# Projection and Gram product as pairs of 64-row matmuls, and gathers that also wait for the slot in front

## The chip, the core and the metric

The kernel runs on one core of a Trainium2 chip, in float32 throughout. The metric is the device time of one execution in microseconds (us), with all inputs in HBM at the start and the 512 outputs in HBM at the end. Five engines work side by side, each through its own list of instructions and tied to the others by semaphores: PE (TensorE, matmuls), DVE (VectorE), ACT (ScalarE), POOL (GpSimd, which issues the gathers here) and SP (SyncE, which issues the other DMAs).

## What is computed

A recommendation tower on 512 samples. For each sample 26 embedding rows of 64 numbers are gathered, projected to 128, normalised, mixed over the 26 features into 32, normalised again, and multiplied pairwise with each other and with a projected dense vector. The products pass a linear layer and an MLP.

```python
e = jnp.stack([tbl_f[ids[:, f]] for f in range(26)], axis=1)        # (512, 26, 64)
x = layer_norm(dense_t @ Wd.T, gd, bd)                              # (512, 128)
y = layer_norm(jnp.einsum('bnd,ed->bne', e, Ws), gs, bs)            # (512, 26, 128)
y = jnp.einsum('bne,pn->bep', y, Wsi)                               # (512, 128, 32)
y = jnp.swapaxes(layer_norm(y, gsi, bsi), 1, 2)
T = jnp.concatenate([x[:, None, :], y], axis=1)                     # 33 rows of 128
Z = jnp.einsum('bnd,bmd->bnm', T, T)                                # lower triangle kept
z = layer_norm(Z[:, TRIL_I, TRIL_J] @ Wl.T, gl, bl)                 # 384 of 512 used
h = relu(concat([z, dense_t]) @ W_top1 + b_top1)
out = relu(h @ W_top2 + b_top2) @ W_top3
```

## The kernel before

The 512 samples are four chunks of 128, a chunk is four slots of 32 samples (16 slots in all, numbered s = 0 to 15). A slot's embedding rows lie in `e_rows` as 4 tiles of 128 rows (slots 0, 4, 8, 12) or 3 tiles (the others). A row of a tile holds two embeddings side by side, a and b (64 numbers each, from samples 16 apart), so that 128 columns are two halves of 64. Each tile takes two gathers on POOL (L373), one for each half: 8 or 6 per slot, 104 in all.

A slot goes through these steps, named by their function:

- `turn` (PE, L432) transposes the slot's tiles into `turn_ps`; `save_cols` (ACT, L673) copies them to `e_cols`.
- `quad` (PE, L451) multiplies `e_cols` by `gram`, a 128x128 matrix with the same 64x64 block twice on its diagonal; `variance_n` (DVE, L882 and L885) multiplies by `e_rows` and sums, which is the norm's variance without the projection itself. `root_n` (ACT, L684) and `norm_n` (DVE, L906 and L910) make `e_unit`.
- `mix` (PE, L440) mixes the features into `mix_ps` (a in partitions 0 to 63, b in 64 to 127); `save_f` (ACT, L680) copies each half to partitions 0 to 63 of its own `f_sb` buffer. Partitions 64 and up of `f_sb` hold a constant, written once, and `proj_w` has the bias in row 64 and zeros below.
- `project` (PE, L474), in the round after, multiplies each half by `proj_w` over all 128 rows: two matmuls of 512 columns into the two banks of `proj_ps`. `square` (ACT, L665), `variance_p` (DVE, L873), `root_p` (ACT, L688), `invert_p` and `norm_p` (DVE, L889 and L897) write the normalised result to `feats`.
- `dots` (PE, L465), one round later still, makes the pairwise products in 32 groups of columns; `save_z` (ACT, L704) stores them. After a chunk SP sends them through HBM back as `z_pairs`, and `linear` (L488) and the MLP follow in later rounds, between the steps above.

Round i of PE is `turn(i)`, `project(i-1)` and `quad(i)` (the two projections stand on either side of `quad`), some work of the linear layers, `mix(i)`, more of that work, `dots(i-2)`. ACT and DVE walk through their lists in the same rounds. All orders are written out by hand. On POOL, the gathers of slot s stand behind `after_round(s-2)`: for s of 4 and more it waits until `dots(s-4)` is done, which is the last thing that PE does in round s-2; for s = 2 and 3 it waits for `mix(s-2)` and for the rows of slot s-1.

The functions named in the diff, with the line numbers of the profile:

## Time and profile before

| | |
|---|---|
| time, median of 3 runs | 193.77 us (193.14 to 194.11) |
| the profiled execution, its own time | 194.12 us |
| its span in the trace | 192.2 us |
| busy in the span: PE / DVE / ACT / POOL | 148.4 / 99.7 / 89.6 / 101.6 us |
| instructions | 4178 |

The span is from the first to the last recorded instruction; about 2 us of the time lie around it. Busy time overlaps between engines, and a share of busy time doesn't say what the end waits for. For that the chain of waits and the timeline are read.

### The profile page before, as it was taken

How to read it: one execution, taken by the hardware profiler on the slowest of the kernel's cores; microseconds unless marked ns; L12 is line 12 of the kernel's file. 1: busy time of each engine (PE TensorE's matmuls, PEld its weight loads, DVE VectorE, ACT ScalarE, POOL GpSimd, SP SyncE). 2: the span in 40 equal slices, each digit the busy share in tenths (PEclk: the TensorE clock that was granted, in tenths of full speed). 3: DMA queues.
4: the chain of work that ended last, by engine and by line, in shares of the span. 5: the costliest groups of instructions: out<-in, count | busy, mean ns of one | idle time of the engine just before them, and what ended most of it. 6: DMA issues, size and time to landing. Idle time of an engine off the chain costs nothing.

```text
span 192.2 us, 4178 instructions
## 1 busy us (share of the span) xinstructions
PE 148.4 (77%) x1644; PEld 96.9 (50%) x1644; DVE 99.7 (52%) x192; ACT 89.6 (47%) x225; POOL 101.6 (53%) x113
## 2 busy tenths in 40 slices
PE   0496496958767976488869867798695889989995
PEld 0343444534444643354457646455565566446674
DVE  2390946684916882838073847361838456541001
ACT  3613043744512566755545436436744546641251
POOL 4777364757874487676375774776757720000000
PEclk9999669999979999969999999999999999999999
DMA  5813131416311015431011155111011640025000
GB/s 143 272 30 76 34 110 26 127 26 211 116 28 22 10 27 129 72 55 27 9 21 20 30 139 80 31 34 20 20 24 27 156 66 3 3 65 106 6 3 0
DMA packets 20260, 11.58 MB, mean 60 GB/s; under 512 B 12945, under 2 KB 17681, under 8 KB 20242
## 3 DMA queue, kind: packets, MB, share of 16 engines
q1 hardware_dynamic: 16226, 7.83, 15.2%
q0 software_dynamic: 3328, 3.41, 10.0%
q8 instruction: 13, 0.21, 0.5%
q10 hardware_dynamic: 688, 0.08, 0.3%
q14 instruction: 5, 0.04, 0.1%
HBM read 9.15 MB, written 2.16 MB: 59 GB/s over the span
## 4 chain that ended last, share of the span: by engine, by line
PE 40%; POOL 20%; DMA 13%; DVE 11%; issue 9%; ACT 5%; SPq 1%; POOLq 1%; DVEq 0%; ACTq 0%
POOL e_rows L373 20%; DMA e_rows<-table_dram,rows_sb 7%; PE mix_ps L440 7%; PE o_ps L488 5%; PE quad_ps L451 5%; PE proj_ps L474 4%; DMA dense_sb<-dense_t_dram 3%; DVE e_unit L910 3%; DVE e_prod L882 3%; DVE var_n L885 3%; PE dots_ps L465 3%; PE turn_ps L432 2%; PE o_ps L403 2%; PE dots_ps L396 2%; PE o_turn_ps L403 2%
## 5 line engine op out<-in xcount | busy, mean ns | idle before, releaser
L373 POOL DMA_INDIRECT e_rows<-table_dram,rows_sb x104 | 100.7, 968 | 53.1 <-issue 27.7
L440 PE MATMUL mix_ps<-mixw_sb,e_unit 128*128 128x192 f32 (+4 forms) x128 | 23.0, 325 | 17.0 <-DVE e_unit L910 17.0
L440 PEld LDWEIGHTS mix_ps<-mixw_sb,e_unit 128*128 128x128 f32 x128 | 20.0, 199 | 25.6 <-DVE e_unit L910 25.6
L882 DVE TENSOR_TENSOR e_prod<-quad_ps,e_rows 128x384 f32<-128x384 f32 (+1 forms) x16 | 9.5, 591 | 45.2 <-PE quad_ps L451 45.2
L474 PE MATMUL proj_ps<-f_sb,proj_w 128*128 128x512 f32 x60 | 32.5, 625 | 0.0
L873 DVE TENSOR_REDUCE var_p<-y_sq 128x16 f32<-128x512 f32 x32 | 20.5, 677 | 1.6 <-ACT y_sq L665 1.6
L451 PEld LDWEIGHTS quad_ps<-gram,e_cols 128*128 128x128 f32 x104 | 14.5, 206 | 12.2 <-ACT e_cols L673 11.2
L680 ACT COPY f_sb<-mix_ps 64x512 f32<-64x512 f32 x32 | 18.5, 578 | 4.5 <-PE mix_ps L440 4.1
L665 ACT ACTIVATE y_sq<-proj_ps 128x512 f32<-128x512 f32 x30 | 17.7, 589 | 5.9 <-PE proj_ps L474 5.7
L432 PE MATMUL turn_ps<-small_sb,e_rows 128*128 128x128 f32 x52 | 9.7, 302 | 13.9 <-DMA e_rows<-table_dram,rows_sb 13.8
L897 DVE TENSOR_TENSOR feats<-proj_ps,rstd_p 128x512 f32<-128x512 f32 x30 | 19.3, 686 | 0.6
L488 PE MATMUL o_ps<-wl_gained,z_pairs 128*128 128x512 f32 (+1 forms) x40 | 18.8, 600 | 0.3 <-DMA z_pairs<-z_dram 0.3
L451 PE MATMUL quad_ps<-gram,e_cols 128*128 128x128 f32 x104 | 15.7, 293 | 1.9 <-ACT e_cols L673 1.9
L684 ACT ACTIVATE std_n<-var_n,eps 128x8 f32<-128x8 f32 x16 | 4.8, 300 | 23.5 <-DVE var_n L885 23.5
L432 PEld LDWEIGHTS turn_ps<-small_sb,e_rows 128*128 128x128 f32 x52 | 6.1, 149 | 17.3 <-DMA e_rows<-table_dram,rows_sb 15.1
L465 PEld LDWEIGHTS dots_ps<-feats 128*32 128x32 f32 x1024 | 10.8, 109 | 7.3 <-issue 5.4
L688 ACT ACTIVATE std_p<-var_p,eps 128x32 f32<-128x32 f32 x16 | 5.1, 322 | 18.0 <-DVE var_p L873 18.0
L673 ACT COPY e_cols<-turn_ps 128x384 f32<-128x384 f32 (+1 forms) x16 | 8.1, 506 | 11.6 <-PE turn_ps L432 11.5
L465 PE MATMUL dots_ps<-feats 128*32 128x33 f32 x1024 | 12.7, 199 | 0.0
L488 PEld LDWEIGHTS o_ps<-wl_gained,z_pairs 128*128 128x128 f32 (+1 forms) x40 | 7.1, 190 | 7.5 <-issue 6.4
L910 DVE TENSOR_TENSOR e_unit<-e_rows,rstd_n 128x384 f32<-128x384 f32 (+1 forms) x16 | 9.6, 597 | 0.6
L885 DVE TENSOR_REDUCE var_n<-e_prod 128x6 f32<-128x384 f32 (+1 forms) x16 | 9.4, 586 | 0.6
(142 smaller groups left out, 172.8 us busy)
## 6 DMA issues: line engine op xcount, KB each, us to landing
z_dram<-z_mine SPq DMA_DIRECT2D x4, 512.0 KB, 3.2
e_rows<-table_dram,rows_sb POOLq DMA_INDIRECT x104, 2.5
w_sb<-w_dram SPq DMA_DIRECT2D x2, 512.0 KB, 6.6
wl_sb<-wl_dram SPq DMA_DIRECT2D x2, 512.0 KB, 3.4
w_sb<-w_dram SPq DMA_DIRECT2D x1, 768.0 KB, 4.2
dense_sb<-dense_t_dram SPq DMA_DIRECT2D x1, 512.0 KB, 5.8
wl_sb<-wl_dram SPq DMA_DIRECT2D x1, 256.0 KB, 2.7
z_pairs<-z_dram SPq DMA_DIRECT2D x4, 64.0 KB, 2.0
```

Of the source, the lines that this page charges most:

```text
L373: pool.indirect_dma_start(out=e_rows[:, chunk, t, D * ab:D * (ab + 1)], out_offset=None, in_=table, in_offset=bass.IndirectOffsetOnAxis(ap ...
L432: mm = pe.transpose(turn_ps[:, P * t:P * (t + 1)], e_rows[:, chunk, t0 + t, :], eye_sb)
L440: mm = pe.matmul(mix_ps[:, PR * at:PR * (at + number)], e_unit[:, t, :], mixw_sb[:, t, lo:lo + number, :].rearrange("k b p -> k (b p)"), s ...
L451: mm = pe.matmul(quad_ps[:, P * t:P * (t + 1)], e_cols[:, q % 2, P * t:P * (t + 1)], gram[:], start=True, stop=True)
L465: mm = pe.matmul(dots_ps[PR * k:PR * (k + 1), (PR + 1) * g:(PR + 1) * (g + 1)], f[:, 2:PR + 2], f[:, 0:PR + 1], start=True, stop=True)
L474: pe.matmul(proj_of(s, ab), proj_w[:], f_sb[:, q % 2, ab, :], start=True, stop=True).then_inc(projected, 1)
L488: mm = pe.matmul(o_ps[:], z_pairs[0:tall, chunk, c, :, :].rearrange("p k g -> p (k g)"), wl_gained[0:tall, c, :], start=(c == 0), stop=(c ...
L665: act.activation(y_sq[:, QB * ab:QB * (ab + 1), :].rearrange("p b q -> p (b q)"), proj_of(s, ab), ACT.Square).then_inc(sq_ready, 1)
L680: act.copy(f_sb[0:D, q % 2, ab, :], mix_ps[D * ab:D * (ab + 1), :]).then_inc(f_ready, 1)
L873: dve.tensor_reduce(var_p[:, QB * ab:QB * (ab + 1)], y_sq[:, QB * ab:QB * (ab + 1), :], AX.X, ALU.add).then_inc(ssq_ready, 1)
L897: dve.tensor_tensor(feats[:, q % 2, QB * ab:QB * (ab + 1), 2:PR + 2], proj_of(s, ab).rearrange("p (b q) -> p b q", q=PR), rstd_p[:, QB * a ...
L910: dve.tensor_tensor(e_unit[:, t0:t0 + nt, :].rearrange("p t (a d) -> p (t a) d", d=D), e_rows[:, chunk, t0:t0 + nt, :].rearrange("p t (a d ...
```

## The change

The two halves a and b are kept in different partitions throughout, so that each is multiplied over 64 rows of the array and needs no zeros:

- `save_f` becomes one copy of 128 partitions. `project` is two matmuls over partitions 0 to 63 and 64 to 127, side by side in the program, ahead of `quad`. Since no row is left for the bias, it is put into the banks first and the matmuls add to it (`start=False`): the new `seed(s)` on ACT copies the constant `y_seed` into both banks of `proj_ps` once `norm_p(s-1)` has read them, and `project(s)` waits for that. For slot 0, two matmuls with the identity do it.
- `quad` is two matmuls of 64 columns per tile, half a into `quad_ps` and half b into `turn_ps`; `variance_n` reads them in two products, and `turn` waits for these.
- The last slot's projection goes to `proj_ps` as the others, behind `dots(14)`. The setup has fewer small copies and fills.
- On POOL, the gathers of every slot from 4 on wait, beside `dots`, for the rows of the slot in front to have landed.

```diff
-        f_sb = sb("f_sb", [P, 2, 2, 512])
+        f_sb = sb("f_sb", [P, 2, 512])
+        y_seed = sb("y_seed", [P, 512])
...
@@ gpsimd
                 elif i >= 0:
                     pool.wait_ge(mixed, i + 1)
-                    pool.wait_ge(gathered[0][i + 1], 32 * tiles_of(i + 1)[1])
+                if i >= 0:
+                    chunk, q = place(i + 1)
+                    pool.wait_ge(gathered[chunk][q], 32 * tiles_of(q)[1])
...
@@ tensor, turn
                 wait(pe, cols_ready, s)
+                wait(pe, prod_done, s)
...
@@ tensor, quad
                 for t in range(nt):
-                    mm = pe.matmul(quad_ps[:, P * t:P * (t + 1)], e_cols[:, q % 2, P * t:P * (t + 1)], gram[:],
-                                   start=True, stop=True)
+                    for ab in range(2):
+                        half = slice(D * ab, D * (ab + 1))
+                        mm = pe.matmul(quad_half_ps[ab][:, D * t:D * (t + 1)], e_cols[half, q % 2, P * t:P * (t + 1)],
+                                       gram[half, :], start=True, stop=True)
                 mm.then_inc(quad_done, 1)
...
-            def project(s, ab):
+            def project(s):
+
                 _, q = place(s)
-                if s < SLOTS - 1:
-                    wait(pe, y_ready, 2 * s - 1 + ab)
-                pe.wait_ge(f_ready, 2 * s + ab + 1)
-                pe.matmul(proj_of(s, ab), proj_w[:], f_sb[:, q % 2, ab, :], start=True,
-                          stop=True).then_inc(projected, 1)
+                pe.wait_ge(f_ready, s + 1)
+                if s == 0:
+                    pe.wait_ge(prep_act, 7)
+                    for ab in range(2):
+                        pe.matmul(proj_ps[:, ab, :], eye_sb, y_seed[:], start=True, stop=True)
+                wait(pe, seeded, 2 * s)
+                for ab in range(2):
+                    half = slice(D * ab, D * (ab + 1))
+                    pe.matmul(proj_ps[:, ab, :], proj_w[half, :], f_sb[half, q % 2, :], start=False, stop=True,
+                              skip_group_check=True).then_inc(projected, 1)
...
@@ tensor, rounds
                 turn(i)
                 if i >= 1:
-                    project(i - 1, 0)
+                    project(i - 1)
                 quad(i)
-                if i >= 1:
-                    project(i - 1, 1)
...
             linear(CHUNKS - 2, range(1, 2))
-            project(last, 0)
-            project(last, 1)
             dots(last - 1)
+            project(last)
             linear(CHUNKS - 2, range(2, KZ))
...
@@ scalar
-                for ab in range(2):
-                    act.copy(f_sb[0:D, q % 2, ab, :], mix_ps[D * ab:D * (ab + 1), :]).then_inc(f_ready, 1)
+                act.copy(f_sb[:, q % 2, :], mix_ps[:]).then_inc(f_ready, 1)
+
+            def seed(s):
+
+                for ab in range(2):
+                    act.wait_ge(y_ready, 2 * (s - 1) + ab + 1)
+                    act.copy(proj_ps[:, ab, :], y_seed[:]).then_inc(seeded, 1)
...
                 if i == 10:
                     relu_2_early(0)
+                if i >= 1:
+                    seed(i)
                 if 2 <= i < SLOTS - 2:
                     save_z(i - 2)
...
             save_f(last)
+            seed(last)
             square(last, 0)
...
@@ vector, variance_n
-                dve.tensor_tensor(e_prod[:, 0:2 * nt, :].rearrange("p a d -> p (a d)"), quad_ps[:, 0:P * nt],
-                                  e_rows[:, chunk, t0:t0 + nt, :].rearrange("p t d -> p (t d)"), ALU.mult).then_inc(prod_done, 1)
+                for ab in range(2):
+                    last_prod = dve.tensor_tensor(e_prod[:, 0:2 * nt, :].rearrange("p (t a) d -> p a t d", a=2)[:, ab, :, :],
+                                           quad_half_ps[ab][:, 0:D * nt].rearrange("p (t d) -> p t d", d=D),
+                                           e_rows[:, chunk, t0:t0 + nt, D * ab:D * (ab + 1)], ALU.mult)
+                last_prod.then_inc(prod_done, 1)
```

PE's row for round 2, before. `turn_ps` is the transpose's bank, `proj_ps` the projection's, and the names in brackets are the semaphores waited for:

```order
L432 MATMUL turn_ps<-small_sb,e_rows 128x128 [waits cols_ready,gathered0_2]
L432 MATMUL turn_ps<-small_sb,e_rows 128x128 x2
L474 MATMUL proj_ps<-f_sb,proj_w 128x512 [waits f_ready,y_ready]
L451 MATMUL quad_ps<-gram,e_cols 128x128 [waits var_ready,cols_ready]
L451 MATMUL quad_ps<-gram,e_cols 128x128 x2
L474 MATMUL proj_ps<-f_sb,proj_w 128x512 [waits f_ready,y_ready]
L440 MATMUL mix_ps<-mixw_sb,e_unit 128x96 [waits f_ready,unit_ready]
```

The same place now:

```order
L431 MATMUL turn_ps<-small_sb,e_rows 128x128 [waits prod_done,cols_ready,gathered0_2]
L431 MATMUL turn_ps<-small_sb,e_rows 128x128 x2
L481 MATMUL proj_ps<-f_sb,proj_w 128x512 [waits seeded,f_ready]
L481 MATMUL proj_ps<-f_sb,proj_w 128x512
L452 MATMUL quad_ps<-gram,e_cols 128x64 [waits var_ready,cols_ready]
L452 MATMUL turn_ps<-gram,e_cols 128x64
...
L439 MATMUL mix_ps<-mixw_sb,e_unit 128x96 [waits f_ready,unit_ready]
```

The second projection has moved ahead of `quad`, `quad` has twice the matmuls, and the wait for `y_ready` has become one for `seeded`, which stands on ACT behind `y_ready`.

ACT's row from the end of round 7 into round 8, before (`o_sq`, `o_std` and `o_unit` normalise the linear layer's output of a chunk, and `e_cols` is `save_cols(8)`):

```order
L680 COPY f_sb<-mix_ps 64x512 [waits projected,mixed]
L680 COPY f_sb<-mix_ps 64x512
L727 ACTIVATE o_sq,o_var<-o_ps 128x512 [waits o_done]
L731 ACTIVATE o_std<-o_var,eps 128x1 [waits osq_done]
L735 ACTIVATE o_unit<-o_ps,o_rstd 128x384 [waits orstd_done]
L704 COPY z_mine<-dots_ps 128x33x8 [waits dotted]
L673 COPY e_cols<-turn_ps 128x512 [waits quad_done,turned]
```

And now:

```order
L678 COPY f_sb<-mix_ps 128x512 [waits projected,mixed]
L731 ACTIVATE o_sq,o_var<-o_ps 128x512 [waits o_done]
L735 ACTIVATE o_std<-o_var,eps 128x1 [waits osq_done]
L739 ACTIVATE o_unit<-o_ps,o_rstd 128x384 [waits orstd_done]
L684 COPY proj_ps<-y_seed 128x512 [waits y_ready] x2
L708 COPY z_mine<-dots_ps 128x33x8 [waits dotted]
L672 COPY e_cols<-turn_ps 128x512 [waits quad_done,turned]
```

Two copies of 64 partitions are one of 128, and two new copies stand between `o_unit` and the copy of the next slot's transposes.

POOL's gathers of slots 4 to 7, before:

```order
L373 DMA e_rows<-table_dram,rows_sb 128x64 [waits dotted]
L373 DMA e_rows<-table_dram,rows_sb 128x64 x7
L373 DMA e_rows<-table_dram,rows_sb 128x64 [waits dotted]
L373 DMA e_rows<-table_dram,rows_sb 128x64 x5
L373 DMA e_rows<-table_dram,rows_sb 128x64 [waits dotted]
L373 DMA e_rows<-table_dram,rows_sb 128x64 x5
```

And now (`gathered1_0` counts what has landed of chunk 1's first slot, slot 4):

```order
L371 DMA e_rows<-table_dram,rows_sb 128x64 [waits gathered0_3,dotted]
L371 DMA e_rows<-table_dram,rows_sb 128x64 x7
L371 DMA e_rows<-table_dram,rows_sb 128x64 [waits gathered1_0,dotted]
L371 DMA e_rows<-table_dram,rows_sb 128x64 x5
L371 DMA e_rows<-table_dram,rows_sb 128x64 [waits gathered1_1,dotted]
L371 DMA e_rows<-table_dram,rows_sb 128x64 x5
```

The first gather of each slot has one more semaphore to wait for.

## Rows read from the trace of the kernel before

**Rows 1.** The waits: engine, line, releaser: us in total, times, longest.

```profile
POOL e_rows L373 <- PE dots_ps L465: 17.6, 10, 4.2
PE turn_ps L432 <- DMA e_rows<-table_dram,rows_sb: 13.8, 10, 2.9
```

**Rows 2.** The timeline of POOL: start, us, operation; gathers at ends of slots 6 to 8.

```profile
71.17 0.94 POOL L373 DMA_INDIRECT e_rows<-table_dram,rows_sb  x1 [0.30 <-issue]
72.42 0.94 POOL L373 DMA_INDIRECT e_rows<-table_dram,rows_sb  x1 [0.30 <-issue]
...
78.66 0.94 POOL L373 DMA_INDIRECT e_rows<-table_dram,rows_sb  x1 [0.30 <-issue]
80.47 0.94 POOL L373 DMA_INDIRECT e_rows<-table_dram,rows_sb  x1 [0.86 <-PE dots_ps L465]
...
89.41 0.94 POOL L373 DMA_INDIRECT e_rows<-table_dram,rows_sb  x1 [0.30 <-issue]
```

**Rows 3.** The instructions of line 373: time from issue to landing.

```profile
DMA to landing us min/median/max: 2.3/2.5/3.6
```

**Rows 4.** The timeline of PE, round 6 and the start of round 7.

```profile
73.66 0.55 PE L432 MATMUL turn_ps<-small_sb,e_rows 128*128 128x128 f32 x3 [1.91 <-DMA e_rows<-table_dram,rows_sb]
74.04 1.02 PE L474 MATMUL proj_ps<-f_sb,proj_w 128*128 128x512 f32 x2
74.90 0.83 PE L451 MATMUL quad_ps<-gram,e_cols 128*128 128x128 f32 x6
...
78.14 1.36 PE L440 MATMUL mix_ps<-mixw_sb,e_unit 128*128 128x96 f32 x8 [1.54 <-DVE e_unit L910]
79.43 0.77 PE L465 MATMUL dots_ps<-feats 128*32 128x33 f32 x64
82.26 0.90 PE L432 MATMUL turn_ps<-small_sb,e_rows 128*128 128x128 f32 x3 [2.07 <-DMA e_rows<-table_dram,rows_sb]
```

**Rows 5.** Groups by line and form: count, busy us, mean ns, idle before.

```profile
L474 PE MATMUL proj_ps<-f_sb,proj_w 128*128 128x512 f32 x60 | 32.5, 625 | 0.0
L451 PE MATMUL quad_ps<-gram,e_cols 128*128 128x128 f32 x104 | 15.7, 293 | 1.9 <-ACT e_cols L673 1.9
L680 ACT COPY f_sb<-mix_ps 64x512 f32<-64x512 f32 x32 | 18.5, 578 | 4.5 <-PE mix_ps L440 4.1
L440 PE MATMUL mix_ps<-mixw_sb,e_unit 128*128 128x64 f32 x16 | 3.2, 287 | 1.4 <-DVE e_unit L910 1.4
L882 DVE TENSOR_TENSOR e_prod<-quad_ps,e_rows 128x384 f32<-128x384 f32 x12 | 6.7, 558 | 30.2 <-PE quad_ps L451 30.2
L882 DVE TENSOR_TENSOR e_prod<-quad_ps,e_rows 128x512 f32<-128x512 f32 x4 | 2.8, 692 | 15.0 <-PE quad_ps L451 15.0
```

**Rows 6.** The timeline of ACT and of PE in round 2.

```profile
36.84 0.47 ACT L673 COPY e_cols<-turn_ps 128x384 f32<-128x384 f32 x1
37.36 0.94 PE L451 MATMUL quad_ps<-gram,e_cols 128*128 128x128 f32 x6
```

**Rows 7.** The timeline of ACT in round 8: the copy of the transposes.

```profile
95.21 0.60 ACT L673 COPY e_cols<-turn_ps 128x512 f32<-128x512 f32 x1
```

**Rows 8.** The timeline of PE: the transposes of slots 4, 8, 12 and 15.

```profile
54.64 0.96 PE L432 MATMUL turn_ps<-small_sb,e_rows 128*128 128x128 f32 x4 [2.90 <-DMA e_rows<-table_dram,rows_sb]
...
93.85 0.63 PE L432 MATMUL turn_ps<-small_sb,e_rows 128*128 128x128 f32 x4
...
131.44 0.66 PE L432 MATMUL turn_ps<-small_sb,e_rows 128*128 128x128 f32 x4 [0.54 <-DMA e_rows<-table_dram,rows_sb]
...
157.44 0.55 PE L432 MATMUL turn_ps<-small_sb,e_rows 128*128 128x128 f32 x3 [0.74 <-DMA e_rows<-table_dram,rows_sb]
```

**Rows 9.** Granted clock (PEclk) from 51 to 58 us, and PE's projection there.

```profile
51.00:58.00 7.00, 4.10 (x69) 2.81 (x56) 2.40 (x3) 2.31 (x5) 5.48 (x6) 0.78 0.16 33
...
55.39 1.92 PE L474 MATMUL proj_ps<-f_sb,proj_w 128*128 128x512 f32 x2
```

**Rows 10.** The timeline of ACT in the tail: the last slot's second square.

```profile
166.21 0.60 ACT L665 ACTIVATE y_sq<-quad_ps 128x512 f32<-128x512 f32 x1 [0.26 <-PE quad_ps L474]
```

More of the change, by code:

```diff
@@ L151, in tower @@
         moment_ps = o_ps[0:TALL, :]
+        quad_half_ps = [quad_ps, turn_ps]
         h1_early_ps = [o_turn_ps, o_turn_ps, quad_ps]
@@ L157, in tower @@
         y_last_ps = dots_ps[0:1, 0:P]
-        proj_last_ps = [turn_ps[:], quad_ps[:]]
         ids_sb = sb("ids_sb", [P, 2, CHUNKS * TILES * 2], I32)
@@ L380, in _ @@
             pe.wait_ge(small_in, 16)
-            pe.wait_ge(consts, 5)
+            pe.wait_ge(consts, 3)
             pe.wait_ge(prep_dve, 2)
@@ L601, in _ @@
             turn(last)
-            project(last - 1, 0)
+            project(last - 1)
             quad(last)
-            project(last - 1, 1)
             dots(last - 2)
@@ L634, in _ @@
             act.wait_ge(prep_pe, 1)
-            for half in range(2):
-                for ab in range(2):
-                    last = act.copy(f_sb[D:P, half, ab, :].rearrange("p (b q) -> p b q", q=PR),
-                                    quad_ps[D:P, 0:PR].unsqueeze(1).to_broadcast([P - D, QB, PR]))
-            last.then_inc(prep_act, 1)
+            act.activation(y_seed[:].rearrange("p (b q) -> p b q", q=PR), quad_ps[:, 0:PR].unsqueeze(1).to_broadcast([P, QB, PR]),
+                           ACT.Copy, scale=bs_sb[:, 0:1]).then_inc(prep_act, 1)
             act.wait_ge(prep_pe, 2)
             act.copy(ws_rows[:], turn_ps[:, 0:D].unsqueeze(1).to_broadcast([P, 2, D])).then_inc(prep_act, 1)
-            act.activation(ws_grows[:], turn_ps[:, 0:D], ACT.Copy, scale=gs_sb[:, 0:1]).then_inc(prep_act, 1)
+            act.activation(ws_grows[:], turn_ps[:, 0:D].unsqueeze(1).to_broadcast([P, 2, D]), ACT.Copy,
+                           scale=gs_sb[:, 0:1]).then_inc(prep_act, 1)
             act.wait_ge(prep_pe, 3)
-            act.copy(gram[0:D, 0:D], mix_ps[0:D, 0:D])
-            act.copy(gram[D:P, D:P], mix_ps[D:P, 0:D]).then_inc(prep_act, 1)
+            act.copy(gram[:], mix_ps[:, 0:D]).then_inc(prep_act, 1)
             act.wait_ge(prep_pe, 4)
-            act.copy(proj_w[D:D + 1, :], ws_sb[D:D + 1, :])
-            act.copy(proj_w[0:D, :], o_turn_ps[0:D, 0:EW]).then_inc(prep_act, 1)
+            act.copy(proj_w[:], o_turn_ps[:, 0:EW]).then_inc(prep_act, 1)
             act.wait_ge(prep_pe, 5)
@@ L665, in square @@
                 act.activation(y_sq[:, QB * ab:QB * (ab + 1), :].rearrange("p b q -> p (b q)"),
-                               proj_of(s, ab), ACT.Square).then_inc(sq_ready, 1)
+                               proj_ps[:, ab, :], ACT.Square).then_inc(sq_ready, 1)
             def save_cols(s):
@@ L1037 @@
     put("eye", np.eye(P, dtype=np.float32))
-    put("ws", np.concatenate([a["L0_rec_Ws"].T, a["L0_rec_bs"][None]]))
+    put("ws", a["L0_rec_Ws"].T)
     put("wsi", a["L0_rec_Wsi"].T)
     put("gs", columns(a["L0_rec_gs"]))
+    put("bs", columns(a["L0_rec_bs"]))
     put("gd", columns(a["L0_rec_gd"]))
```

24 lines of the change are left out of this document (10 added, 14 removed).

## The prediction

> **What bounds the kernel now.** I read the chain that ended last, the waits, and then the timelines of POOL, PE and ACT round by round. The chain passes from POOL to DMA to PE and back in nearly every slot, and what ties them is a loop. POOL waits ten times for `dots`, 17.6 us in all, and PE's `turn` waits ten times for landed rows, 13.8 us [rows 1]. So neither engine is the bound alone: the gathers of slot s start when PE ends round s-2, and PE's round s starts when they have landed.
>
> The lengths in this loop: a gather takes 1.25 us from start to start, so 6 of them span 6.24 us (72.42 to 78.66) and 8 span 8.94 (80.47 to 89.41) [rows 2]. The last lands 2.5 us after its start, 3.6 at most [rows 3]; slot 7's were such, issued at 78.66 and used at 82.26 [rows 2, 4]. A light round of PE is 6.5 us long: `turn` at 73.66, `dots` over at 80.20, and then 2.07 us of waiting for rows [rows 4]. What lies in the round between `quad` and `mix` is DVE's and ACT's work on the variance, not PE's.
>
> **The wait on POOL.** At present the gathers of slot 7 start 1.25 us after the last gather of slot 6 (71.17, 72.42), those of slot 8 1.81 us after the last of slot 7 [rows 2]. With the new wait this gap can't be under landing and wake-up. POOL starts 0.27 us after the `dots` that releases it (80.20 to 80.47) [rows 2, 4], so the gap is 2.5 + 0.3 = 2.8 us, or 3.9 where the landing takes 3.6. What is queued behind this wait is all of the slot's gathers, and `turn` waits for these. The shortest period of a slot becomes 6.3 + 2.8 = 9.1 us with 3 tiles, 8.9 + 2.8 = 11.7 with 4, and about 1.1 more after a slow landing (slots 7 and 11, while `z_pairs` is read). Nothing hides it: issue and landing used to overlap between slots and no longer do. This floor is hit wherever PE's round is shorter, which light rounds of 6.5 us are.
>
> **The projection.** Two records of 512 columns take 0.86 us (74.04 to 74.90), once per half [rows 4]. The trace has no 64-row matmul. Bounds for the pair: 0.86 us if they run side by side, 1.72 if one after the other. The nearest row is `dots`, 32 matmuls into four separate column groups: 64 records in 0.77 us [rows 4]. Six records of `quad`, 128 columns each, last 0.83 us and one of them 0.29 [rows 4, 5], so they start 0.11 us apart; one of 33 columns would take 0.03 by that, and 64 in line 1.8 us. So small matmuls in different parts of the array do overlap here, and I take 0.86. `quad(i)` then starts as before, behind one matmul's length, since `save_cols` ends about then. The 0.86 us saved behind `quad` lay beside DVE's variance work: no gain on the path.
>
> The Trainium skill ("TensorE: Matmul & The Clock Gate", Part 3) states that matmuls on different row groups run concurrently, and so would give the pair 0.86 too; no row of this trace shows it for rows. Against the change stands "TensorEngine Tiling (Array Packing)", Key Properties: switching the tiling mode drains the TensorE. Two more switches per round come in. The trace shows no visible gap at such a switch now: `dots` starts at 79.43, inside the modelled end of `mix` at 79.50 [rows 4]. By the rule I would put 0.18 us on each switch, an estimate from what the last record of `quad` lasts beyond the distance of two (0.29 less 0.11), and 1.4 us on eight switches in four rounds bound by work.
>
> **The Gram product.** Matmuls of 64 columns on 128 loaded columns: `mix` has such a form, with a mean of 287 ns against 293 of the 128 columns in `quad` [rows 5]. So half the columns gain next to nothing there, and I read this as the loading of the weights being the longer side. Four records per tile in place of two: 0.22 us per tile as now if the halves' loads overlap, 0.44 if not, 0.11 if the shorter moving side counts in full. I take 0.22, no change, which the concurrency seen in `dots` supports. The two products on DVE cost more: 384 elements take 558 ns and 512 take 692, so 1.05 ns an element and 156 ns fixed [rows 5]; a second instruction adds up to 0.16 us, less about 0.06 of overlap between neighbours: 0.1 us per slot on the path of the round.
>
> **The seeds on ACT.** `save_f` loses one copy of 0.58 us, `seed` adds two of about 0.59 [rows 5]: 0.6 us more per round. Its place matters more. `seed(i)` waits for `norm_p(i-1)` and stands ahead of `save_cols(i+1)`, so the next round's `e_cols`, `quad` and DVE's variance are queued behind it, and `project` waits for it too. Where PE waits for rows anyway (light rounds) that is hidden. In rounds that follow at once it shows:
>
> - Round 1: two seed matmuls at 0.86 us ahead of `quad(1)`: 1.7 us.
> - Round 2: `e_cols` starts at 36.84, directly behind other work of ACT, and `quad` at 37.36 [rows 6]. Now two seed copies (1.2 us) come first, then `project` (0.86) and only then `quad`: 36.84 + 1.2 + 0.1 + 0.86 = 39.0, so 1.6 us later.
> - Rounds 7 to 8 and 11 to 12: `e_cols` starts at 95.21, 1.4 us after PE's `turn` at 93.85, held by ACT's work on the linear layer's output [rows 7, 8]; the two seed copies come in ahead of it: 1.2 us later, each time where the floor doesn't cover it.
>
> **The sum**, by stretches between the transposes at 54.64, 93.85, 131.44 and 157.44 [rows 8]:
>
> - up to slot 4: 1.7 + 1.6 + 0.2 for the products = **+3.5**; the landing wait of slot 3 is covered by it.
> - slots 4 to 8, 39.2 us now: 9.1 + 9.1 + 10.2 + 12.0 (round 7 with `linear`, bound by work a little over its floor of 11.7) = 40.4, **+1.2**.
> - slots 8 to 12, 37.6 now: 10.9 (round 8: 9.5 and the seeds 1.2 and products 0.1) + 9.1 + 10.2 + 11.7 = 41.9, **+4.3**.
> - slots 12 to 15, 26.0 now: 9.3 + 9.1 + 9.7 (slot 15 lands after 3.1) = 28.1, **+2.1**.
> - the tail: the last slot's second square starts at 166.21 [rows 10]. It is now behind one copy (0.6 less), two seeds (1.2 more), and the first square which no longer overlaps a matmul (0.6 later, less 0.2); with the products **+1.0**.
> - together **+12.1 us**.
>
> **The clock.** From 51 to 58 us the granted clock is 0.78 of full, which is a time at the lower level of 1.2 GHz, after PE waited 2.90 us for rows; the projection took 1.92 us there and 1.02 elsewhere, and the round lost 1.7 us in all [rows 4, 8, 9]. With periods at the floor PE waits some 2.6 us in every light round and works less before it. I expect more such stretches. A light round has the room for one (6.5 + 1.7 is under 9.1), the work-bound rounds 2, 7, 8 and 12 have not. I take one more in these, 1.7 us, and with some spread **+2.0**.
>
> So 194.12 + 12.1 + 2.0 = 208.2 on the profiled execution; that one was 0.35 us above the median, so about **208**.
>
> **The rivals.**
>
> - *The halves don't run side by side.* The change then doesn't do what it says: `project` stays at 1.72 us, now all ahead of `quad`, and `quad` may double. Where work binds (rounds 1, 2, 3, 7, 8, 11, 12, 15) 0.86 us each, or 0.22 per tile: +7 to +9, so 215 to 217. For it: no 64-row matmul in the trace. Against: `dots`.
> - *The small ends of the unknown costs.* `quad` at 0.11 per tile saves 0.35 us in each work-bound round, about 3; landings at 2.3 us [rows 3] save 0.2 a slot, about 2; no more low clock, 2: 201.
> - *Faster than before.* POOL waits for `dots` ten times now [rows 1]. If what bounds a slot stays the end of PE's round and not the landing, each round shorter by the projection's 0.86 us starts the next gathers earlier: 11 rounds, 9.5 us, less the 3.5 of the start: 188. It decides where the gap from the last gather to the next first one, 2.8 by my count, is under what PE leaves, so only if rows land in about 1 us. The rows say 2.3 at least [rows 3], and the saved matmul isn't on the round's path.
> - *The wait is absorbed and the seeds hidden*: ACT is busy for 89.6 of 192.2 us. Then the start's 1.7 and the products' 0.1 per slot stay: 197. Against it: ACT's order, not its load, delays.
>
> **How the numbers follow.** My forecast with its own range, 203 to 213: 0.56. Serial halves, 213 to 220: 0.17. Small ends, 199 to 203: 0.17. Absorbed: 0.05. Faster: 0.03, and a draw, between the last two, 0.02. The range that leaves out no more than 2 in 10 goes from 200 to 217. Half a per cent, 1 us, is about what a measurement of this kernel can tell from no change. Faster 0.03, same 0.02, slower 0.95.
>
> **What would show it.** On POOL the gap between slots, last start to first start, at 2.8 us or more everywhere and its waits ended by landed rows instead of by `dots`; `turn` to `turn` at 9.1 us in light rounds; `proj_ps` records of both halves starting within a few ns and the pair over in 0.9 us; `quad_ps` and `turn_ps` together at 0.22 per tile; `e_cols` in rounds 2 and 8 directly behind the copies of `y_seed`; PEclk with more low places than before. The forecast is wrong if gathers got faster one by one, if pairs took 1.7 us, or if PE's low clock took much more than 2 us.

## The result, and the profile after

The changed kernel is slower by 13%: 223.25 us, median of 4 runs (219.97 to 225.67), against 193.94 (193.14 to 196.00) for the kernel before on the same chip, ratio 1.131 (95% interval 1.118 to 1.145). The forecast was 208, with a range from 200 to 217. Some executions of each kernel take longer at a lower granted clock, and the ratios leave these out: of the changed kernel two (225.6 and 225.7 us, clock 0.817, the profiled one among them) beside three that count, 218.4 to 220.9 us (0.836 to 0.866). Differences are judged by ratios, and 1% is 1.9 us.

The page of the kernel after, its granted clock (tenths of full, 40 slices of 5.6 us) and the chain that ended last by engine:

```profile
span 223.3 us, 4417 instructions
...
PE 167.1 (75%) x1752; PEld 114.8 (51%) x1752; DVE 100.3 (45%) x208; ACT 94.8 (42%) x234; POOL 99.8 (45%) x111
...
PEclk9997596959956996558758955969559997999999
...
PE 48%; DVE 14%; ACT 10%; DMA 10%; POOL 9%; issue 7%; POOLq 1%; SPq 1%; DVEq 0%
```

The mean granted clock is 0.817; before it was 0.964. The clock is at either full speed (2.4 GHz) or half, so the time at the low level is 2 x (1 - clock) x span: 81.7 us of this execution against 13.8 before. In the row of the 40 slices 19 are under 9; before there were five, in three stretches. The three executions that count have 64.9 us of it in the mean.

The waits (engine, line, releaser: us in total, times, longest):

```profile
POOL e_rows L371 <- PE dots_ps L466: 35.0, 7, 6.8
...
POOL e_rows L371 <- DMA e_rows<-table_dram,rows_sb: 12.5, 5, 3.5
PE turn_ps L431 <- DMA e_rows<-table_dram,rows_sb: 11.2, 6, 2.8
...
PE proj_ps L481 <- ACT proj_ps L684: 7.3, 6, 1.7
```

POOL's new wait ended last only 5 times. Seven times POOL waited for `dots`, 35.0 us in all, where it was 17.6 in ten waits [rows 1]. The loop is the same, but now PE's round is its longer side. And `project` has a new wait, for the seeds.

PE's timeline, rounds 4 to 7 and the start of round 8 (start, us, operation, idle before it and its releaser):

```profile
60.26 0.66 PE L431 MATMUL turn_ps<-small_sb,e_rows 128*128 128x128 f32 x4 [2.83 <-DMA e_rows<-table_dram,rows_sb]
60.84 1.96 PE L481 MATMUL proj_ps<-f_sb,proj_w 64*128 64x512 f32 x4
62.59 0.31 PE L452 MATMUL quad_ps<-gram,e_cols 64*128 64x64 f32 x1
62.60 0.31 PE L452 MATMUL turn_ps<-gram,e_cols 64*128 64x64 f32 x1
...
72.09 0.55 PE L431 MATMUL turn_ps<-small_sb,e_rows 128*128 128x128 f32 x3
72.56 1.13 PE L481 MATMUL proj_ps<-f_sb,proj_w 64*128 64x512 f32 x4
73.52 0.22 PE L452 MATMUL quad_ps<-gram,e_cols 64*128 64x64 f32 x1
73.53 0.22 PE L452 MATMUL turn_ps<-gram,e_cols 64*128 64x64 f32 x1
...
81.09 0.55 PE L431 MATMUL turn_ps<-small_sb,e_rows 128*128 128x128 f32 x3 [1.38 <-DMA e_rows<-table_dram,rows_sb]
...
90.69 0.90 PE L431 MATMUL turn_ps<-small_sb,e_rows 128*128 128x128 f32 x3 [0.77 <-DMA e_rows<-table_dram,rows_sb]
92.76 2.08 PE L481 MATMUL proj_ps<-f_sb,proj_w 64*128 64x512 f32 x4 [1.17 <-ACT proj_ps L684]
...
105.65 0.66 PE L431 MATMUL turn_ps<-small_sb,e_rows 128*128 128x128 f32 x4
108.03 1.37 PE L481 MATMUL proj_ps<-f_sb,proj_w 64*128 64x512 f32 x4 [1.73 <-ACT proj_ps L684]
```

The halves do run side by side: the two halves of `quad` start 10 ns apart, and `quad` starts 0.96 us after the start of the projection's pair, four records, at full clock (72.56 to 73.52), 1.8 us at the low one (60.84 to 62.59). These rows hold a light round at full clock (72.09 to 81.09, 9.0 us) and one in which the clock was mostly low (90.69 to 105.65, 15.0 us). The windows of round 4, of these two and of round 8, with their granted clock (third number from the end):

```profile
60.30:72.10 11.80, 10.89 (x101) 6.46 (x101) 6.64 (x13) 4.11 (x10) 5.66 (x6) 0.57 0.09 17
72.10:81.10 9.00, 6.14 (x102) 3.68 (x96) 4.80 (x10) 5.54 (x13) 5.66 (x6) 1.00 0.13 24
...
90.70:105.70 15.00, 13.37 (x102) 7.82 (x102) 5.07 (x11) 5.76 (x15) 7.55 (x8) 0.62 0.16 26
105.70:119.70 14.00, 10.24 (x114) 8.72 (x112) 5.33 (x11) 7.29 (x19) 5.66 (x6) 0.63 0.09 15
```

Between the same transposes as in [rows 8], in us; the right column is e3, the changed kernel with extra matmuls that raise the clock (below):

| stretch | before | after | more | my sum | e3, more |
|---|---|---|---|---|---|
| to `turn(4)` | 54.6 | 60.3 | +5.6 | +3.5 | 0.0 |
| `turn(4)` to `turn(8)` | 39.2 | 45.4 | +6.2 | +1.2 | +4.1 |
| `turn(8)` to `turn(12)` | 37.6 | 47.7 | +10.1 | +4.3 | +5.1 |
| `turn(12)` to `turn(15)` | 26.0 | 32.9 | +6.9 | +2.1 | +3.0 |
| the tail | 34.8 | 37.0 | +2.2 | +1.0 | +2.8 |
| together | 192.2 | 223.3 | +31.1 | +12.1 | +15.0 |

### The profile page after: what moved, and what is told of

Its sections match the earlier page's. It is cut to its first block, busy times and chain, and to the rows that moved or that the text cites. A ratio compares the mean times of both kernels' runs of the same rounds, so it can differ in the third digit from the quotient of the medians.

```text
span 223.3 us, 4417 instructions
## 1 busy us (share of the span) xinstructions
PE 167.1 (75%) x1752; PEld 114.8 (51%) x1752; DVE 100.3 (45%) x208; ACT 94.8 (42%) x234; POOL 99.8 (45%) x111
## 3 DMA queue, kind: packets, MB, share of 16 engines
q1 hardware_dynamic: 16226, 7.83, 13.1%
## 4 chain that ended last, share of the span: by engine, by line
PE 48%; DVE 14%; ACT 10%; DMA 10%; POOL 9%; issue 7%; POOLq 1%; SPq 1%; DVEq 0%
PE mix_ps L439 12%; POOL e_rows L371 9%; PE proj_ps L481 8%; PE o_ps L495 6%; DMA e_rows<-table_dram,rows_sb 5%; PE quad_ps L452 5%; DVE e_prod L890 4%; DVE e_unit L920 3%; DVE var_n L895 3%; ACT proj_ps L684 3%; PE o_turn_ps L522 2%; DMA dense_sb<-dense_t_dram 2%; PE dots_ps L466 2%; PE o_ps L401 2%; PE dots_ps L394 2%
## 5 line engine op out<-in xcount | busy, mean ns | idle before, releaser
L439 PE MATMUL mix_ps<-mixw_sb,e_unit 128*128 128x192 f32 (+4 forms) x128 | 32.9, 423 | 24.8 <-DVE e_unit L920 24.8
L439 PEld LDWEIGHTS mix_ps<-mixw_sb,e_unit 128*128 128x128 f32 x128 | 29.1, 273 | 33.6 <-DVE e_unit L920 33.6
L890 DVE TENSOR_TENSOR e_prod<-quad_ps,e_rows 128x192 f32<-128x192 f32 (+1 forms) x16 | 6.0, 375 | 72.3 <-PE turn_ps L452 72.3
L481 PE MATMUL proj_ps<-f_sb,proj_w 64*128 64x512 f32 x64 | 22.4, 780 | 7.3 <-ACT proj_ps L684 7.3
L452 PEld LDWEIGHTS quad_ps<-gram,e_cols 64*128 64x128 f32 x104 | 18.6, 244 | 10.7 <-ACT e_cols L672 6.8
L452 PEld LDWEIGHTS turn_ps<-gram,e_cols 64*128 64x128 f32 x104 | 18.6, 244 | 0.0
L431 PE MATMUL turn_ps<-small_sb,e_rows 128*128 128x128 f32 x52 | 10.1, 313 | 11.2 <-DMA e_rows<-table_dram,rows_sb 11.2
L452 PE MATMUL quad_ps<-gram,e_cols 64*128 64x64 f32 x104 | 17.6, 320 | 1.1 <-ACT e_cols L672 1.1
L684 ACT COPY proj_ps<-y_seed 128x512 f32<-128x512 f32 x30 | 17.0, 590 | 2.1 <-DVE feats L907 2.0
L452 PE MATMUL turn_ps<-gram,e_cols 64*128 64x64 f32 x104 | 17.6, 320 | 0.0
L678 ACT COPY f_sb<-mix_ps 128x512 f32<-128x512 f32 x16 | 9.3, 583 | 13.2 <-PE mix_ps L439 13.2
```

Source lines behind the costliest of these rows:

```text
L431: mm = pe.transpose(turn_ps[:, P * t:P * (t + 1)], e_rows[:, chunk, t0 + t, :], eye_sb)
L439: mm = pe.matmul(mix_ps[:, PR * at:PR * (at + number)], e_unit[:, t, :], mixw_sb[:, t, lo:lo + number, :].rearrange("k b p -> k (b p)"), s ...
L452: mm = pe.matmul(quad_half_ps[ab][:, D * t:D * (t + 1)], e_cols[half, q % 2, P * t:P * (t + 1)], gram[half, :], start=True, stop=True)
L481: pe.matmul(proj_ps[:, ab, :], proj_w[half, :], f_sb[half, q % 2, :], start=False, stop=True, skip_group_check=True).then_inc(projected, 1)
L684: act.copy(proj_ps[:, ab, :], y_seed[:]).then_inc(seeded, 1)
L890: last_prod = dve.tensor_tensor(e_prod[:, 0:2 * nt, :].rearrange("p (t a) d -> p a t d", a=2)[:, ab, :, :], quad_half_ps[ab][:, 0:D * nt]. ...
```

## The experiments

The medians of the kernel before on the same chip: for e1 to e4 193.55 us, e5 to e8 192.18, e9 to e12 193.88, e13 to e16 192.16. Where a kernel has no ratio, only its fastest execution would count in one, and that one is given.

**First: is it the structure or the clock?** The theory: the change costs my 12 us of structure and the rest is a low clock in PE's lighter rounds. The rival: nearly all of it is structure (the seeds), and the clock only mirrors PE's waiting.

**e1_before_poolwait**: the kernel before, with POOL's wait alone.

```
+                if i >= 0:
+                    chunk, q = place(i + 1)
+                    pool.wait_ge(gathered[chunk][q], 32 * tiles_of(q)[1])
```

> The kernel before with only the new wait on POOL: the gathers of every slot also wait for the rows of the slot in front. Theory 1 (the clock explains most of the loss, and the clock falls because PE has less to do in its rounds and waits longer between them): the wait alone costs the 7 us of its floor (9.1 and 11.7 us per slot), a little more if low clock comes with the idle time: 201 to 204 us. Theory 2 (the gather wait is the main cause): 212 us or more.

Measured: 202.05 us (201.43 to 205.61), ratio 1.055 (1.045 to 1.064), clock 0.949. Its waits:

```profile
POOL e_rows L375 <- DMA e_rows<-table_dram,rows_sb: 30.2, 13, 3.1
```

Thirteen waits end with landed rows, as the forecast described; the wait costs the kernel before 8.5 us by the medians, 10.5 by the ratio.

**e2_after_nowait**: the changed kernel with POOL's waits as they were before.

> The changed kernel with the new wait on POOL taken out again, all else as changed. Theory 1: the seeds, the pairs and the low clock stay, so 2 to 5 us less than the changed kernel, 214 to 218 us, with a granted clock that is still under 0.87 on average. Theory 2 (the wait is the main cause): back to about 200 us.

Measured: 218.09 us (212.24 to 224.29), ratio 1.113 (1.100 to 1.127), clock 0.816 in the profile. The ratio falls by 1.8 points, 3.5 us, within the intervals. So the wait is worth less here than alone, and most of what made the forecast wrong is in the other edits.

**e3_after_fill**: the changed kernel with one or two more matmuls per round ahead of `mix`, into `mix_ps`, which `mix` then overwrites. They are 19 matmuls in all, each of which makes two records in the trace.

```
+                wait(pe, f_ready, i)
+                for _ in range(1 if i in (3, 4, 5, 7, 8, 9, 10, 11, 12, 13, 14) else 2):
+                    pe.matmul(mix_ps[:], wd_c[:, 0, :], dense_sb[:, 0, :], start=True, stop=True)
                 mix(i)
```

> The changed kernel with filler on PE: ahead of each mix, where PE waits for e_unit, one or two matmuls of 128x128 by 512 columns whose result is overwritten. Nothing of the computation is left out. Theory 1: PE's clock stays at its upper level for most of the span (mean above 0.93) and the time falls to what the sum without the clock gave, 206 to 211 us, though more work is done. Rival (the loss is in the waits on ACT and POOL, and the clock only follows from it): the time stays at 218 to 226 us or rises by the filler's 20 us.

Measured: 208.61 us (207.87 to 209.20), ratio 1.088 (1.079 to 1.096), clock 0.934. The page, the transposes that open PE's rounds 7 to 10, and the window of round 8:

```profile
PE 162.7 (79%) x1790; PEld 103.5 (50%) x1790; DVE 100.4 (48%) x208; ACT 94.7 (46%) x234; POOL 100.8 (49%) x111
...
PEclk9996999699889978999579999996999996999999
...
L574 PE MATMUL mix_ps<-dense_sb,wd_c 128*128 128x512 f32 x38 | 23.3, 720 | 0.0
...
86.01 0.55 PE L431 MATMUL turn_ps<-small_sb,e_rows 128*128 128x128 f32 x3 [1.93 <-DMA e_rows<-table_dram,rows_sb]
97.95 0.66 PE L431 MATMUL turn_ps<-small_sb,e_rows 128*128 128x128 f32 x4 [1.06 <-DMA e_rows<-table_dram,rows_sb]
109.27 0.55 PE L431 MATMUL turn_ps<-small_sb,e_rows 128*128 128x128 f32 x3
118.38 0.55 PE L431 MATMUL turn_ps<-small_sb,e_rows 128*128 128x128 f32 x3 [1.55 <-DMA e_rows<-table_dram,rows_sb]
...
97.95:109.27 11.32, 10.39 (x114) 7.43 (x114) 5.17 (x10) 6.52 (x17) 6.15 (x6) 0.70 0.10 19
```

19 useless matmuls (38 records), 23.3 us of PE's time, make the kernel faster by 4.4 points, 8.5 us (14.6 by the medians). PE's total busy time even falls, from 167.1 to 162.7, since everything else on it runs faster. The light round 9 (109.27 to 118.38) is at 9.1 us, the floor of my forecast, and ends in a wait for rows. Rounds 7 and 8 together take 23.3 us (86.01 to 109.27), where the changed kernel takes 29.0. This is the strongest evidence for the clock.

**e4_before_fill**: one such matmul in rounds 0, 1, 2 and 6 of the kernel before.

> The kernel before with one filler matmul (128x128 by 512 columns, overwritten) ahead of mix in rounds 0, 1, 2 and 6. A control for the filler. Theory 1: there are three low stretches in the kernel before, which cost some 2 us each in the loop; if the filler lifts one or two of them the time is 190 to 194 us, and it is not over 196. Rival (filler in these gaps costs its own length): 197 us.

Measured: 192.38 us (189.34 to 194.95), ratio 0.995 (0.987 to 1.003). There is next to nothing to win back where the clock is high already.

**Second: what lowers the clock, and by which path do the seeds cost?**

**e5_reorder**: e2 with the seeds behind `save_cols` on ACT and `quad` ahead of `project` on PE; `root_n` also stands ahead of `square`.

```
                 turn(i)
+                quad(i)
                 if i >= 1:
                     project(i - 1)
-                quad(i)
...
                 save_cols(i)
+                if i >= 2:
+                    seed(i - 1)
...
-                if i >= 1:
-                    seed(i)
```

> The changed kernel without its new wait on POOL, and with the seeds out of the way: seed(i-1) stands behind save_cols(i) on ACT, quad(i) ahead of project(i-1) on PE. If the low clock comes from PE's lighter rounds (halves side by side), it stays: mean granted clock under 0.87 and 211 to 218 us, a few us under the 218 of the same kernel with the old order. If it comes from PE waiting for the seeds, the clock is back over 0.93 and the time at 196 to 203.

Measured: 207.53 us (202.64 to 208.51), the fastest 202.64 at a clock of 0.915, the others at 0.867 and 0.868. All lie under all of e2's (212.24 and more): a gain of some 10 us, more than I expected with the clock still low.

**e6_reorder_fill**: e5 with e3's filler.

> The kernel of e5_reorder with one or two extra 512-column matmuls per round ahead of mix, as in e3_after_fill. Theory of the clock: 3 to 4 us (seeds, order) and 8 us (POOL's wait) under e3's 208.6, so 196 to 201, clock over 0.93. If extra work of PE is on the path here and the clock was not what cost, 212 or more.

Measured: 210.08 us (208.50 to 213.91), ratio 1.090 (1.076 to 1.103), clock 0.918. A miss: the clock rose, but less than in e3, and no execution is under e5's best. In this order the filler brings no gain that can be told. That its own time costs what the clock brings is argued and not shown; I did not find which of its matmuls stand on the path.

**e7_no_seed**: the changed kernel without seeds. The bias is left out, and `project` starts its banks anew.

```
-                wait(pe, seeded, 2 * s)
+                wait(pe, y_ready, 2 * s)
...
-                    ... f_sb[half, q % 2, :], start=False, stop=True,
+                    ... f_sb[half, q % 2, :], start=True, stop=True,
```

> The changed kernel with the seeds left out: project starts its PSUM banks anew, so the bias bs is not added; everything else stays, POOL's wait too. Lighter rounds as the cause: the granted clock stays under 0.88, and the time falls by the structure of the seeds alone, my 1.7 + 1.6 + 1.2 + 1.2 of the prediction and not more than 7, so 216 to 221. PE's wait for the seeds as the cause of the low clock: clock over 0.93 and 204 to 210.

Measured: 210.12 us (209.48 to 211.12), ratio 1.091 (1.082 to 1.099), clock 0.861. Neither theory as written: the clock stays low, as the first said, and the ratio falls by 4.1 points, 7.8 us (13.1 by the medians), a little over the bound of 7 that I gave.

**e8_whole_quad**: the changed kernel with `quad` as before, one 128-column matmul per tile and one product on DVE, for which `turn` no longer waits.

> The changed kernel with the Gram product as before: one matmul of 128 rows and 128 columns per tile, one product on DVE. The halved projection, the seeds and POOL's wait stay. If it is the time in which PE works that counts for the clock, nothing comes back, since quad takes 0.22 us per tile either way: 219 to 225, clock 0.80 to 0.86. If half-filled matmuls count as less work for the clock, part of the 15 us comes back: 211 to 218 and clock over 0.88.

Measured: 216.56 us (216.18 to 218.54), ratio 1.128 (1.117 to 1.139), clock 0.905. The ratio is that of the changed kernel within 0.3 points: nothing is shown to come back, although the profiled execution has only 40.8 us at the low level. The clock and the median are those that I expected if half-filled matmuls count for less (over 0.88, 211 to 218): with `quad` whole the four executions have 0.890 to 0.912, the changed kernel 0.866 at most. So the Gram halves lower the clock, but what comes back of the clock doesn't come back in time, and a low stretch doesn't cost the same everywhere.

**Third: each part alone, and the seeds at a high clock.**

**e9_pair_alone**: the projection in halves and the single copy of `save_f`; no seeds (bias left out), `quad` whole, no new wait.

> Of the whole change only the projection as two matmuls of 64 rows and the single copy of save_f: no seeds (so the bias bs is not added), Gram product whole, no new wait on POOL. If the pair costs no clock by itself, the 0.86 us saved per round lies off the path: 190 to 194 us, granted clock over 0.93. If the shorter projection already lowers the clock: 0.88 to 0.92 and 196 to 201.

Measured: 199.35 us (194.39 to 201.98), the fastest 194.39 at 0.964; the kernel before took 193.1 in the mean of the five that count. No gain. By the fastest no loss can be told either, but the three others lie at 198.5 and more (clock 0.923 to 0.948), above every execution of the kernel before (195.0 at most), so a loss isn't excluded.

**e10_quad_halves**: the kernel before with `quad` in halves.

```
+                    for ab in range(2):
+                        half = slice(D * ab, D * (ab + 1))
+                        mm = pe.matmul(quad_half_ps[ab][:, D * t:D * (t + 1)], e_cols[half, q % 2, P * t:P * (t + 1)],
+                                       gram[half, half], start=True, stop=True)
```

> The kernel before with only the Gram product in two 64-row matmuls per tile (and two products on DVE; the next transposes wait for them). By my prediction 0.1 us a slot: 194 to 196, clock over 0.93. If the halves lower the clock by themselves: clock 0.85 to 0.92 and 198 to 204.

Measured: 196.32 us (192.98 to 196.44), the fastest 192.98 at 0.973, the others at 196.3 to 196.4. No loss in the fastest; the forecast's 0.1 us a slot is neither shown nor refuted.

**e11_no_seed_fill**: e7 with e3's filler.

> The kernel of e7_no_seed (bias left out) with the filler matmuls of e3_after_fill. Theory 1, seeds cost 4 to 7 us by their place and the rest of the 13 us between after and e7 was clock: 202 to 205, clock over 0.93. Theory 2, the seeds cost 13 us by their place alone, at any clock: 196 to 199. Theory 3, the filler helps only by covering a stretch that the seeds open: no gain over e7's 210.

Measured: 205.84 us (205.02 to 207.94), ratio 1.068 (1.058 to 1.078), clock 0.949. With the filler the seeds cost 2.0 points, 3.8 us (e3 against e11); without it 4.1 points, 7.8 us. So perhaps half of what they cost comes with the low clock: the two differences lie 2.1 points apart, which their intervals hardly tell from nothing. The time is just above the 202 to 205 of the first theory; the second (196 to 199) and the third (no gain) are out.

**e12_half_fill**: e3 with the filler on 64 rows.

```
+                    pe.matmul(mix_ps[:], wd_c[0:D, 0, :], dense_sb[0:D, 0, :], start=True, stop=True)
```

> The kernel of e3_after_fill with the filler matmuls on 64 rows instead of 128, same columns, same number, so the same time on PE. If only PE's time at work counts for the granted clock, as in e3: 207 to 211 us, clock over 0.92. If half-filled matmuls count for less, clock 0.82 to 0.89 and 212 to 222.

Measured: 216.27 us (213.03 to 221.34), ratio 1.112 (1.095 to 1.129), clock 0.904. Its page:

```profile
PEclk9996799999999969997579996597589999999999
...
L574 PE MATMUL mix_ps<-dense_sb,wd_c 64*128 64x512 f32 x38 | 24.7, 754 | 0.0
```

The same 19 matmuls (38 records) take about the same time (24.7 us against 23.3) but bring back 2.0 points, 3.8 us, where full ones brought 8.5, and the clock is 0.904 against 0.934. The intervals of e12 and of the changed kernel overlap, those of e12 and e3 hardly (1.095 and 1.096): no execution of e12 is under 213.0 us, none of e3 over 209.2. So it isn't the place or the length of the filler that helps. With the same place and length on half the rows it does less, and the clock is lower. The time is in the range that I gave for half-filled matmuls counting less, the clock above it.

**Fourth, on what was still open.**

**e13_quad_first**: e2 with `quad(i)` ahead of `project(i-1)`, seeds as they are. **e14_seed_late**: e2 with the seeds behind `save_cols`, `project` still ahead of `quad`.

> The kernel of e2_after_nowait (218.1 us) with quad(i) ahead of project(i-1) on PE; the seeds stay where they are. e5_reorder had this and the seeds moved, and took 207.5. If it is quad (and the variance behind it) queued behind the project that waits for the seeds, this move brings nearly all: 207 to 211. If it is the seeds ahead of e_cols on ACT, it brings little: 214 to 219.

> The kernel of e2_after_nowait with only the seeds moved behind save_cols on ACT; project stays ahead of quad on PE. Seeds ahead of e_cols as the cause: 207 to 211. Quad behind project as the cause: 215 to 222, since project waits for its seeds still longer.

Measured: e13 211.88 us (210.90 to 212.69), ratio 1.106 (1.094 to 1.118), clock 0.862, between my two ranges. e14 238.60 us (234.57 to 239.11), clock 0.798: its fastest execution is 10 us over e2's slowest and 22 over its fastest, far over either range. The waits of `quad` in e13, those of `project` in e14, and e14's `e_cols` with the round's seeds on ACT:

```profile
PE quad_ps L450 <- ACT e_cols L670: 17.3, 16, 2.6
PE proj_ps L479 <- ACT proj_ps L682: 28.1, 14, 2.7
...
98.88 0.48 ACT L670 COPY e_cols<-turn_ps 128x384 f32<-128x384 f32 x1
99.25 1.11 ACT L682 COPY proj_ps<-y_seed 128x512 f32<-128x512 f32 x2
...
100.51 1.43 PE L479 MATMUL proj_ps<-f_sb,proj_w 64*128 64x512 f32 x4 [2.67 <-ACT proj_ps L682]
```

PE's order is the path: `quad` and all of DVE's variance work are queued behind a `project` that waits for seeds. In e14 it waits for them 14 times, 28.1 us. Taking `quad` alone out of that queue (e13) brings 0.7 points, which is no gain that can be told, and with the seeds moved as well some 10 us (e5). So each of the two causes that I set against each other holds the other in place: with the seeds ahead of `e_cols`, an early `quad` waits for `e_cols` instead (17.3 us in e13); with them behind, a `quad` behind `project` waits longer. One rival stays untested: e5 alone also has `root_n` ahead of `square`, and what that adds to its gain isn't known.

**e15_halves_only**: both halves, no seeds (bias left out), no new wait.

> The halves of projection and Gram product without seeds (bias left out) and without POOL's new wait. The pair alone took 199.4 us, the Gram halves alone 196.3, before 193.9. If their costs add: 200 to 203, clock about 0.90 to 0.93. If the granted clock falls only when both are there: clock under 0.88 and 204 to 209, that is nearly the 210.1 of e7, which also has POOL's wait.

Measured: 205.40 us (203.93 to 210.34), ratio 1.067 (1.053 to 1.081), clock 0.845 in the profile and 0.89 in the median. Both halves together cost 6.7%, 13 us. In the fastest execution of each, neither half alone costs anything that can be told (e9, e10), and the clock is 0.964 with the pair, 0.973 with the Gram halves, against 0.896 in the mean with both. So their costs seem not to add. That rests on one execution of each: by the medians the halves alone cost 5.5 and 2.4 us, which is 7.9 of the 13.2 that e15 costs by its own.

**e16_nowait_fill**: e3 without POOL's new wait.

> The changed kernel without POOL's new wait and with the filler of e3_after_fill (208.6 us). If POOL's wait is what is left of the structure at a high clock, it is worth the 8 us that it cost on the kernel before: 199 to 203. If other things bind (seeds, the filler itself, which may be why e6 took 210), 205 to 209.

Measured: 203.61 us (201.30 to 205.31), ratio 1.055 (1.041 to 1.070), clock 0.941. The wait is worth 3.2 points here, 6.3 us: between the 3.5 at the low clock and the 10.5 of e1. With PE's rounds short it shows more, as the forecast's floor has it. The time is just over the 199 to 203 that I gave for the wait as all that is left, so a little else binds too.

**All runs together.** Each execution has its span and its clock. Over the 110 executions of these 18 kernels, each compared with the mean of its own kernel, one more us at the low level goes with 0.30 us more span (correlation 0.89). Over the 64 that count in ratios, of the 14 kernels with two or more, it is 0.16 us (0.63); that choice leaves out the longest executions and so may flatten the slope. The price is thus an estimate from 0.16 to 0.30, and it is a correlation: what else goes with a low clock is in it. With 0.30, and means over the executions that count:

| kernel | executions | span | low time | span less 0.30 x low time |
|---|---|---|---|---|
| before (beside e5 to e8) | 6 | 190.6 | 13.1 | 186.6 |
| POOL's wait alone (e1) | 3 | 200.0 | 22.8 | 193.2 |
| both halves alone (e15) | 3 | 202.9 | 42.2 | 190.2 |
| no seeds (e7) | 4 | 208.4 | 54.6 | 192.0 |
| after | 3 | 217.7 | 64.9 | 198.3 |

By this estimate the changed kernel is 11.6 us longer with no low clock at all, and 52 us more of it make the other 15.5. At 0.16 the split is 18.8 and 8.3, which is nearer to what the filler gives back. The price is a mean over places. e8 doesn't fit (span 215.1, low time 42.6, so 202.3): by it, a whole `quad` would be 4 us longer at full clock than halves, which nothing that I read explains. So the split is known only within these bounds.

No version here beats the kernel before by more than the measurement tells (e4 comes to 0.995).

## Why the prediction was wrong

**The term that failed is "The clock", +2.0 us.** Its mechanism was right in the main: more low stretches, and they cost in rounds bound by work. Its size was wrong. I took one more such stretch, at 1.7 us. In the profiled execution the low time rose by 68 us (52 between the means of the table), some twenty times the 3.1 us that the window of [rows 9] holds (7 us at 0.78). The price that I used, 1.7 us for 3.1 of low time, was not too small; the number of stretches was. The filler gives back 8.5 us and is itself not free, and the estimate from all runs has 8 to 16: in place of +2.0 the term is 8 to 16 us.

**The structure, +12.1, is wrong in its parts and perhaps too small in sum.** The estimate from all runs gives 11.6 to 18.8. e3, whose clock is nearly that of before, is 8.8% longer than the kernel before on its own chip, 17 us, with the filler's cost and some low clock still in it. That it took 208.6 us where I had 208 is partly luck: my 208 was 7.3% over the kernel before, clock included. By stretches e3 has 0.0 where I had +3.5 and +4.1 where I had +1.2. More than half of that gap is round 4: I counted it as light, 9.1 us, and it took 11.8 (60.26 to 72.09) at a clock of 0.57, and 10.9 with the filler. It wasn't light before either: it took 9.8 us, from 54.64 [rows 8] to

```profile
64.39 0.55 PE L432 MATMUL turn_ps<-small_sb,e_rows 128*128 128x128 f32 x3
```

How much the structure lacks in all stays open. Two of its terms are also added up wrong by 0.1, in opposite directions (round 8's parts make 10.8 and the tail's 1.1).

**Why there were so many.** I reasoned that only light rounds would wait more. I overlooked that the change takes work from PE in every round, about 0.86 us of projection, and that waits for seeds come on top. I had also called a light round's low stretch covered "(6.5 + 1.7 is under 9.1)". Round 4, 11.8 us at a clock of 0.57 with PE busy for 10.9 of it, shows that it isn't always. And a low clock outlasts its round: the windows above show 0.62 and 0.63 through rounds 7 and 8, which are bound by work and lost some 3 us each beyond my count (15.0 for 12.0 and 14.0 for 10.9). With the filler the two take 23.3 us together, near the 22.9 of my count, although the clock is 0.70 in round 8. e15 shows that the two halves together lower the clock without any seeds (0.896). Without the seeds the changed kernel's clock is a little higher (e7: 0.869 in the mean against 0.851, with ranges that overlap), and with the filler their absence changes nothing in it (e11), so what the seeds do to the clock isn't settled. Why the clock falls, these runs don't prove. Two of them point the same way: 64-row work leaves a lower clock than 128-row work of the same length in e12, and a whole `quad`, in the same 0.22 us per tile, a higher one than its halves (e8).

**POOL's wait: right.** The gap between the last gather of a slot and the first of the next is never under the floor. POOL's timeline:

```profile
78.66 0.94 POOL L371 DMA_INDIRECT e_rows<-table_dram,rows_sb  x1 [0.30 <-issue]
81.80 0.94 POOL L371 DMA_INDIRECT e_rows<-table_dram,rows_sb  x1 [2.19 <-DMA e_rows<-table_dram,rows_sb]
```

3.1 us (78.66 to 81.80) where my count said 2.8, and light rounds of 9.0 us (72.09 to 81.09) where it said 9.1. It costs 3.5 us in the changed kernel (within the intervals), 6.3 with the filler and 10.5 alone: the shorter PE's rounds, the more of the floor shows. I had not taken up that a low clock, by lengthening rounds, hides part of it.

**The projection: right, and off the path.** The pair takes 0.96 us, near the lower bound of 0.86 and far from 1.72. The Trainium skill ("TensorE: Matmul & The Clock Gate", Part 3) says that matmuls on different row groups run concurrently; the trace agrees, by the same 0.96 us. The Trainium skill ("TensorEngine Tiling (Array Packing)", Key Properties) also says that changing the tiling mode drains the TensorE. My estimate for that was 1.4 us; the trace shows at most the 0.1 us by which the pair is longer than one 128-row matmul, and the pair starts at 72.56, inside the modelled end of `turn` (72.64).

**The Gram product: right.** Its 0.22 us per tile stands: from 73.52 on the records of each half start 0.11 us apart, two per tile. My 0.1 us a slot for the second product is below what e10 and e8 can tell.

**The seeds: right in place and about right in price.** In round 2 they stand where I put them, directly ahead of `e_cols`:

```profile
39.49 1.10 ACT L684 COPY proj_ps<-y_seed 128x512 f32<-128x512 f32 x2
40.52 0.48 ACT L672 COPY e_cols<-turn_ps 128x384 f32<-128x384 f32 x1
```

My terms for them (1.7, 1.6, 1.2, 1.2) make 5.7 us. The filled kernels say 3.8, the table 6.3 at full clock (198.3 less 192.0), and with the low clock it is 7.8. e14 shows how much hangs on `project` waiting ahead of `quad`. I named that queue in round 2 alone; in the trace `project` waits for seeds six times, 7.3 us.

**The rivals.** Serial halves would have given 215 to 217, nearer to the result, but for a reason that the trace refutes. The faster and the absorbed case are both out. The case that happened, something near my structure with a clock that collapses, I had named only among what would make the forecast wrong.

## What to carry to other kernels

Before a change that takes work off PE or makes PE wait, price the clock as well: look how close the kernel is to low stretches now, and count with many of them; here each us at the low level went with 0.16 to 0.30 us, an estimate for these kernels. If PE's busy time rises although its work was cut (167 us here), compare the mean granted clock first; extra matmuls into a bank that is overwritten are a cheap test of whether the clock is the cause. Don't put a matmul that waits for another engine's preparation ahead of one that starts a long chain, and move the preparation with it: here either move alone gained nothing or cost much (e13, e14), both together some 10 us (e5).

## What the runs showed that I had not expected

- 19 useless matmuls of 128 rows, 23.3 us of PE's time, make the changed kernel 8.5 us faster (clock 0.817 to 0.934 in the profiles).
- Halving the projection brings nothing even alone (e9: 194.4 us in its fastest execution, against 193.1 in the mean before).
- Costs of small edits on PE seem not to add: none in the fastest executions of each alone, 13 us together (e15).
- A whole `quad` raises the clock (0.851 to 0.901 in the mean) and yet brings no time back by the ratio (e8).
- One kernel varies with its low time: e2 took from 212 to 224 us, with clocks from 0.887 to 0.816.
- PE's busy time rose from 148.4 to 167.1 us though its work was cut; at the higher clock of e3 it is 162.7 with the filler and 139.4 without the filler's 23.3.
